# Row transposes by DMA, masks by ScalarE and new orders in a decoder layer of one core

## The chip, the core and the metric

The kernel runs on one core of a Trainium2 chip. TensorE, VectorE, ScalarE, GpSimd and SyncE each run their own list of instructions in order and meet at semaphores; TensorE writes to eight PSUM banks of 128 x 512 f32, and SyncE's list here only issues DMAs. The metric is the device time of one execution in microseconds. The kernel before takes 849.58 us, the median of 3 runs (848.94 to 849.9).

## What is computed

A decoder layer on x of 8 x 128 x 512, f32, with the normalisation behind each residual sum:

```python
x = _layernorm(x + _L0_attn_ref(x, Wq, bq, ..., Wo, bo), axis=-1)       # 32 heads of 16, causal
x = _layernorm(x + _L0_xattn_ref(x, ctx, ctx, mask, wq, wk, wv, wo), axis=-1)  # 32 query, 8 key heads of 128, rotary
x = _layernorm(x + _L0_ffn_ref(x, gate..., up..., down...), axis=-1)    # 4-bit weights, 1376 wide, f16 result
```

Products are made in f16 from a high and a low half of each operand (three matmuls in place of one), so that each f32 tensor is split: the high half is a cast, the low half the difference.

## The kernel before, in words

**Tiles.** Every engine's program is a loop over tile numbers t. Self-attention has STEPS1 = 64 tiles (t = 0 to 63: eight blocks j of 8 tiles; one tile is 4 heads of one batch of half the rows). T0 = 70 begins cross-attention, 64 tiles v = t - T0 of one batch and one group of 4 query heads, 16 blocks of 4. END = T0 + 64 begins the feed-forward part: four early gate and up products, then the coded tiles (weights of 7 of 11 column groups multiplied as codes), then the down products, batch by batch.

**Self-attention tile t.** TensorE: `scores1(t)` puts the causal mask into a bank by a matmul of a bf16 identity with the bf16 table `tri` (start=True) and adds two score matmuls; then projections of later blocks, or a fill; `weigh1(t - 3)`; `turn1(t - 1)` (four f32 transposes of the probabilities); every second tile one transpose of a normalised result. VectorE: row maximum of t, low half of the probabilities of t - 2 (`p1_lo`), normalisation of a result, then weights, then what the fills of tile t left in their bank. ScalarE: exponentials of t (they wait for the row maximum), high half of the probabilities of t - 1 (`p1_hi`), then projections and fills.

**Fills** (`fill_plan`, line 63) are projections, one or two a tile, that go to banks 0 and 1 in turn; fill f waits until fill f - 2 was consumed (`fill_free`). Kind "o" is the self-attention's output product of a batch (VectorE adds it to `res` and takes the statistics), "t" turns a batch's normalised rows into the columns `aTh`, `aTl` by four f32 transposes of TensorE, a cast by ScalarE and a subtraction by VectorE; "k", "v", "q" are the cross-attention's projections of a block; a "k" or "q" is rotated: VectorE makes three products (`rotation_parts`), GpSimd their sum (`rotation_sum`), ScalarE and GpSimd its halves, with two buffers. Before, tiles 52 to 58 hold k0; o0; o1; t0, o2; t1, o3; t2, v0; t3; and q0 to q3 follow in tiles 59 to 62, k1 in 63, v1 in 64, the queries of block 1 from 65 on. A "q" waits until the four rows tiles of its half are turned.

**Normalisation.** GpSimd makes the inverse deviation (`inverse_sd`) one tile behind the "o" fill. For batches in SHIFTED (4 to 7 of the first norm) it also makes a shift column, and ScalarE applies both; for the others VectorE does (`normalised`).

**Weights.** GpSimd splits the pieces of the first two cross-attention groups (`split_piece`: scale, cast, subtract) in the slots of QKV_SLOT (tiles 54 to 59 for group 1) and OUT_SLOT (50, 52, 60, 61). Self-attention weights of block 2 are split by ScalarE and VectorE in tiles 2 to 5.

**Joint.** In T0 + 2 stand the fills t4, k2, t5; in T0 + 3 t6 and t7. ScalarE takes t5 out of its bank behind the third exponentials; VectorE behind `o_lo(0)`.

**Down weights.** CODES_SLOT names the tiles in which codes are unpacked (VectorE) and scaled (GpSimd, `scale_codes`); column groups 4 and 5 have their down weights split in the coded tiles (`weights_hi` on ScalarE, `down_lo` on GpSimd).

## Time and profile before

| | |
|---|---|
| median of 3 runs | 849.58 us |
| the profiled execution's own time | 849.92 us |
| its span, first to last instruction | 848.1 us |
| TensorE busy | 98% |
| VectorE, GpSimd, ScalarE busy | 81%, 75%, 63% |
| granted TensorE clock, mean | 0.999 of full |
| DMA | 76.8 MB, 91 GB/s |
| chain that ended last | TensorE 62%, GpSimd 14%, VectorE 7%, ScalarE 7% |

Times in a timeline are microseconds from the start of the span: the start, the length, the engine, the line, what is written from what, how many alike; brackets give idle time ahead of it and what ended it. L356 to L358 are the three matmuls of the helper that all projections use, L1667 the transposes of probabilities, L1655 the causal mask, L1734 the transposed rows, L1155 any low half on VectorE.

### The profile page before, as it was taken

What the parts mean: (1) busy time and instruction counts of PE and PEld (TensorE: products, weight loads), DVE (VectorE), ACT (ScalarE), POOL (GpSimd) and SP (SyncE); (2) the same over time, 40 slices, a digit from 0 to 9 for tenths busy, and PEclk for the clock granted to TensorE, in tenths of its full rate; (3) what the DMA queues carried; (4) which work ended last, traced back from release to release, by engine and by line L of the source; (5) the groups of instructions that cost most, each with busy time, mean ns of one, the idle gap of its engine ahead of it and who ended that gap; (6) DMA issues with size and microseconds to landing.
All of it is one profiled execution on the core that took longest, in us unless ns stands there. A gap on an engine that the chain in (4) does not pass through costs nothing.

```text
span 848.1 us, 17377 instructions
## 1 busy us (share of the span) xinstructions
PE 827.7 (98%) x6125; PEld 465.5 (55%) x6125; DVE 689.2 (81%) x1077; ACT 533.6 (63%) x1560; POOL 632.8 (75%) x563
## 2 busy tenths in 40 slices
PE   9899999999999999999999999999999999999997
PEld 4677777655555554555555555555555644434444
DVE  5688788998688778689788788798889755899897
ACT  5798888554765666576575676665666753777400
POOL 1199999897676686578777677578888633999896
PEclk9999999999999999999999999999999999999999
DMA  7675255103244422434425125213442223230011
GB/s 192 194 256 181 63 160 163 54 18 108 38 95 130 112 39 75 112 39 138 105 38 155 33 40 161 38 26 91 133 93 39 46 42 105 72 110 20 2 48 52
DMA packets 120038, 76.76 MB, mean 91 GB/s; under 512 B 72877, under 2 KB 104336, under 8 KB 119952
## 3 DMA queue, kind: packets, MB, share of 16 engines
q1 hardware_dynamic: 117504, 74.86, 33.5%
q10 hardware_dynamic: 2448, 0.79, 0.5%
q8 instruction: 49, 0.80, 0.4%
q14 instruction: 37, 0.30, 0.1%
HBM read 52.50 MB, written 6.36 MB: 69 GB/s over the span
## 4 chain that ended last, share of the span: by engine, by line
PE 62%; POOL 14%; DVE 7%; ACT 7%; issue 6%; DMA 3%; SPq 0%; POOLq 0%; ACTq 0%; DVEq 0%
PE bank L356 16%; PE bank L358 16%; PE bank L357 16%; POOL rot L647 2%; POOL left L680 2%; PE bank L1667 2%; POOL q2l L653 2%; POOL pn L664 2%; ACT prob L845 2%; POOL prob L657 2%; PE bank L1840 1%; PE bank L1841 1%; PE bank L1760 1%; PE bank L1759 1%; PE bank L1758 1%
## 5 line engine op out<-in xcount | busy, mean ns | idle before, releaser
L657 POOL TENSOR_TENSOR prob<-prob,rden 128x512 f32<-128x512 f32 x64 | 67.8, 1060 | 103.3 <-DVE rden L1318 103.0
L647 POOL TENSOR_TENSOR rot<-rcos,rsin 128x512 f32<-128x512 f32 x80 | 106.5, 1332 | 20.3 <-DVE rsin L1260 19.8
L356 PE MATMUL bank<-aTh,xqh 128*128 128x512 f16 x256 | 97.1, 379 | 1.4 <-DVE rsin L1260 0.9
L356 PE MATMUL bank<-xoh,o2h 128*128 128x512 f16 x256 | 97.1, 379 | 0.1
L357 PE MATMUL bank<-xol,o2h 128*128 128x512 f16 x256 | 97.2, 379 | 0.0
L358 PE MATMUL bank<-xoh,o2l 128*128 128x512 f16 x256 | 97.1, 379 | 0.0
L357 PE MATMUL bank<-aTl,xqh 128*128 128x512 f16 x256 | 97.1, 379 | 0.0
L358 PE MATMUL bank<-aTh,xql 128*128 128x512 f16 x256 | 97.1, 379 | 0.0
L1010 ACT ACTIVATE prob<-bank,ebias 128x128 f32<-128x128 f32 x256 | 90.4, 365 | 2.1
L1260 DVE SCALAR_TENSOR_TENSOR rsin<-bank,sinq 64x512 f32<-64x512 f32 x128 | 88.1, 688 | 1.7
L664 POOL TENSOR_TENSOR pn<-prob,pn 128x512 f16<-128x512 f32 x64 | 84.1, 1315 | 6.8 <-ACT pn L1022 6.6
L653 POOL TENSOR_TENSOR q2l<-rot,q2h 128x512 f16<-128x512 f32 x64 | 82.0, 1282 | 0.0
L890 ACT CAST q2h<-rot 128x512 f16<-128x512 f32 x64 | 39.5, 618 | 61.8 <-POOL rot L647 61.4
L796 ACT ACTIVATE ebias<-nmax 128x4 f32<-128x4 f32 x128 | 27.0, 211 | 79.3 <-DVE nmax L1313 51.1
L845 ACT ACTIVATE prob<-bank,ebias 128x128 f32<-128x128 f32 x256 | 73.0, 368 | 2.1
L1155 DVE SCALAR_TENSOR_TENSOR o2l<-bank,o2h 128x512 f16<-128x512 f32 x64 | 43.5, 680 | 37.1 <-ACT o2h L796 36.8
L1022 ACT CAST pn<-prob 128x512 f16<-128x512 f32 x64 | 39.4, 615 | 52.6 <-POOL prob L657 52.4
L1260 DVE SCALAR_TENSOR_TENSOR rcos<-bank,cosq 128x512 f32<-128x512 f32 x64 | 43.7, 683 | 22.4 <-PE bank L358 22.4
L1179 DVE TENSOR_REDUCE nmax<-bank 128x4 f32<-128x512 f32 x64 | 43.7, 684 | 17.5 <-PE bank L1658 16.9
L1010 ACT ACTIVATION_READ_ACCUMULATOR prob<-bank,ebias 128x1 f32 x256 | 51.9, 203 | 0.0
L1332 DVE SCALAR_TENSOR_TENSOR res<-bank,res 128x512 f32<-128x512 f32 x64 | 43.8, 685 | 8.7 <-PE bank L358 8.3
L1155 DVE SCALAR_TENSOR_TENSOR pT<-bank,pT 128x512 f16<-128x512 f32 x64 | 43.8, 685 | 6.8 <-ACT pT L796 6.3
(224 smaller groups left out, 2652.7 us busy)
## 6 DMA issues: line engine op xcount, KB each, us to landing
tst<-tables SPq DMA_DIRECT2D x11, 768.0 KB, 5.2
xqs<-in_xwq SPq DMA_DIRECT2D x8, 1024.0 KB, 6.6
xos<-in_xwo SPq DMA_DIRECT2D x8, 1024.0 KB, 5.6
qst<-in_fq SPq DMA_DIRECT2D x11, 384.0 KB, 3.4
kstk<-stack SPq DMA_DIRECT2D x48, 64.0 KB, 2.3
qstk<-stack SPq DMA_DIRECT2D x21, 128.0 KB, 2.6
xs<-in_ctxT SPq DMA_DIRECT2D x2, 1024.0 KB, 6.3
res<-in_x SPq DMA_DIRECT2D x1, 2048.0 KB, 8.4
```

Of the source, the lines that this page charges most:

```text
L356: pe.matmul(out_ap, ah, bh, start=first, stop=False)
L357: pe.matmul(out_ap, ah, bl, start=False, stop=False)
L358: return pe.matmul(out_ap, al, bh, start=False, stop=last)
L647: nc.gpsimd.tensor_tensor(rot[:, r % 2, :], rcos[:, r % 2, :], rsin[:, r % 2, :], ALU.add).then_inc(rope_rot, 1)
L653: nc.gpsimd.tensor_tensor(lo, rot[:, r % 2, :], hi, ALU.subtract).then_inc(rope_lo, 1)
L657: nc.gpsimd.tensor_tensor(prob[:, v % 2, :].rearrange("p (h k) -> p h k", h=QH), prob[:, v % 2, :].rearrange("p (h k) -> p h k", h=QH), rd ...
L664: nc.gpsimd.tensor_tensor(pn[:, v % 2, 1, :], prob[:, v % 2, :], pn[:, v % 2, 0, :], ALU.subtract).then_inc(c_pn_lo, 1)
L845: last = nc.scalar.activation(prob[:, u % 2, j * S:(j + 1) * S], bank[2 + u % 2][:, j * S:(j + 1) * S], ACT.Exp, bias=ebias[:, u % 2, j:j ...
L1010: last = nc.scalar.activation(prob[:, v % 2, j * S:(j + 1) * S], bank[2 + v % 2][:, j * S:(j + 1) * S], ACT.Exp, bias=ebias[:, v % 2, j:j ...
L1155: return nc.vector.scalar_tensor_tensor(out=dst, in0=src, scalar=2.0 ** e, in1=hi, op0=ALU.mult, op1=ALU.subtract)
L1260: last = nc.vector.scalar_tensor_tensor(out=as_batches(dst[to, r % 2, :]), in0=as_batches(bank[f % 2][src, :]), scalar=2.0 ** (e - E_X - E_W),
L1332: nc.vector.scalar_tensor_tensor(out=r, in0=bank[6 + v % 2][:, :], scalar=2.0 ** (-E_V2 - E_W), in1=r, op0=ALU.mult, op1=ALU.add).then_inc ...
```

## The change

The four "t" fills of batches 0 to 3 go. Their rows are normalised by ScalarE (SHIFTED now holds all eight batches, so GpSimd makes four more shift columns), split as rows: high half by ScalarE (`split_rows_hi`), low half by VectorE (`split_rows_lo`) at the end of its tile, into a buffer of three places, and SyncE issues two DMA transposes for each batch into `aTh` and `aTl` (`turn_rows`). The first half's query fills wait for these DMAs. The fills become o0 to o3 in tiles 52 to 55, v0 in 56, k0 in 57, none in 58; the rest stays. In tiles 56 to 63 the causal mask is put into the bank by a copy on ScalarE, two tiles ahead and behind the exponentials of the running tile, and TensorE's mask matmul goes. In the opening two of three weight pieces of block 2 go to GpSimd, tiles 1 and 2, and block 1's queries leave their bank ahead of the exponentials of tile 0. In T0 + 2 ScalarE takes t5 out of its bank behind `o_hi(0)`, ahead of the exponentials, and VectorE its low half ahead of `o_lo(0)`. The codes of column group 5 are unpacked and scaled in END + 1 instead of END + 4, and the down weights of groups 4 and 5 split in END + 1 to END + 3 instead of in the coded tiles.

Left out here are declarations of semaphores, the size of `lnsh`, and a condition that keeps the early down weights out of ScalarE's coded loop.

```diff
@@ -58,15 +58,15 @@
 END = T0 + STEPS
+SEEDED = STEPS1 - 8
...
-    plan = [(STEPS1 - 12, "k", (0,)), (STEPS1 - 11, "o", (0,)), (STEPS1 - 10, "o", (1,)), (STEPS1 - 9, "t", (0, 0))]
-    plan += [(STEPS1 - 9, "o", (2,)), (STEPS1 - 8, "t", (0, 1)), (STEPS1 - 8, "o", (3,)), (STEPS1 - 7, "t", (0, 2))]
-    plan += [(STEPS1 - 7, "v", (0,)), (STEPS1 - 6, "t", (0, 3))]
+    plan = [(STEPS1 - 12 + b, "o", (b,)) for b in range(BH)]
+    plan += [(STEPS1 - 8, "v", (0,)), (STEPS1 - 7, "k", (0,))]
@@ -133,7 +133,7 @@
-W1_SLOT = {(3, 0): 7, (3, 1): 9, (3, 2): 10}
+W1_SLOT = {(2, 1): 1, (2, 2): 2, (3, 0): 7, (3, 1): 9, (3, 2): 10}
@@ -146,7 +146,7 @@
 APPLY_SLOT.update({(1, b): T0 + BH * (BLOCK_OF[(G - 1, b // BH)]) + b % BH + 5 for b in range(NB)})
-SHIFTED = [(0, b) for b in range(BH, NB)]
+SHIFTED = [(0, b) for b in range(NB)]
@@ -179,8 +179,9 @@
+DOWN_EARLY = {4: END + 1, 5: END + 2}
 EARLY_GU = {END: 1, END + 2: 2, END + 4: 3}
-CODES_SLOT = {0: T0 + 26, 1: T0 + 48, 2: T0 + 49, 3: T0 + 53, 4: END, 5: END + 4}
+CODES_SLOT = {0: T0 + 26, 1: T0 + 48, 2: T0 + 49, 3: T0 + 53, 4: END, 5: END + 1}
@@ -281,6 +282,9 @@
+        rows = at(155.5, "rows", [P, 3, 2, D], F16)
@@ -449,6 +455,13 @@
                 sp.dma_start(xos[:, :, :], xwo.rearrange("(h p) n -> p h n", p=P)[:, g * QH:(g + 1) * QH, :]).then_inc(xo_in, 16)
+            def turn_rows(b):
+                if b == 0:
+                    sp.wait_ge(v1_psum, BLOCKS)
+                for i, (dst, done) in enumerate(((aTh, rows_hi), (aTl, rows_lo))):
+                    sp.wait_ge(done, b + 1)
+                    sp.dma_start_transpose(dst[:, :, b * S:(b + 1) * S], rows[:, b % 3, i, :]).then_inc(rows_in[b % 3], 16)
@@ -528,6 +541,8 @@
             load_kv(1)
+            for b in range(BH):
+                turn_rows(b)
@@ -583,18 +598,21 @@
-            def split_piece(hi, lo, src, lo_done, e=E_W):
+            def split_piece(hi, lo, src, lo_done, e=E_W, ahead=None):
...
                 pool.wait_ge(piece_hi, pieces_done)
+                if ahead is not None:
+                    pool.wait_ge(lo_done, ahead)
...
                 pool.wait_ge(w1_in, 48 * (c - 1))
-                split_piece(w1h[c][:, i, :, :], w1l[c][:, i, :, :], w1s[0][:, i, :, :], w1_lo)
+                split_piece(w1h[c][:, i, :, :], w1l[c][:, i, :, :], w1s[0][:, i, :, :], w1_lo,
+                            ahead=3 * c + i)
@@ -723,7 +741,7 @@
                 for (norm, b), slot in APPLY_SLOT.items():
-                    if norm == layer and slot == t + 1 and (norm, b) not in SHIFTED:
+                    if norm == layer and slot == t + 1 and (layer == 1 or slot < T0):
@@ -770,11 +788,14 @@
                         inter_lo(n)
+                for i in DOWN_EARLY:
+                    if DOWN_EARLY[i] + 1 == t:
+                        down_lo(i)
...
                 add_left(n, 1)
-                if half == 1 and i in DOWN_SPLIT:
+                if half == 1 and i in DOWN_SPLIT and i not in DOWN_EARLY:
@@ -833,6 +854,14 @@
+            def split_rows_hi(b):
+                act.wait_ge(ln_out, b + 1)
+                if b == 0:
+                    act.wait_ge(v1_psum, BLOCKS - 1)
+                if b >= 3:
+                    act.wait_ge(rows_in[b % 3], 32 * (b // 3))
+                split_hi(rows[:, b % 3, 0, :], res[:, b, :], E_X).then_inc(rows_hi, 1)
@@ -855,6 +884,13 @@
+            def seed_triangle(u):
+                if u == SEEDED:
+                    act.wait_ge(consts_ready, 4)
+                act.wait_ge(exp_done, u - 1)
+                nc.scalar.copy(bank[2 + u % 2][:, :].rearrange("p (h k) -> p h k", h=4),
+                               tri[:, :].unsqueeze(1).to_broadcast([P, 4, S])).then_inc(seeded1, 1)
@@ -960,23 +996,37 @@
             w1_split_hi(0, 2)
+            def scaled_norm(layer, b):
+                e, r = layer * NB + b, res[:, b, :]
+                act.wait_ge(ln_shift, SHIFTED.index((layer, b)) + 1)
+                nc.scalar.activation(r, r, ACT.Identity, scale=lnrs[:, e % 3, :],
+                                     bias=lnsh[:, SHIFTED.index((layer, b)), :]).then_inc(ln_out, 1)
...
                 bank_splits(turned_first(t))
+                if t == 0:
+                    q1_out_f32(1)
...
                     exps1(t)
+                if SEEDED <= t + 2 < STEPS1:
+                    seed_triangle(t + 2)
...
                     p1_hi(t - 1)
+                for layer, b in SHIFTED:
+                    if APPLY_SLOT[(layer, b)] == t:
+                        scaled_norm(layer, b)
+                        split_rows_hi(b)
...
                         w1_split_hi(1, i)
-                if j + 1 < BLOCKS and n == 0 and t >= -TILES1:
+                if j + 1 < BLOCKS and n == 0 and t >= -TILES1 and t != 0:
@@ -984,20 +1034,14 @@
                     bring_first_queries()
-                if t in (2, 3, 4):
-                    w1_split_hi(2, t - 2)
+                if t == 2:
+                    w1_split_hi(2, 0)
...
                 rotations(fills_at(t - 1))
-            def scaled_norm(layer, b):
-                e, r = layer * NB + b, res[:, b, :]
-                act.wait_ge(ln_shift, SHIFTED.index((layer, b)) + 1)
-                nc.scalar.activation(r, r, ACT.Identity, scale=lnrs[:, e % 3, :],
-                                     bias=lnsh[:, SHIFTED.index((layer, b)), :]).then_inc(ln_out, 1)
@@ -1097,6 +1141,7 @@
                     o_hi(0)
+                    turned_hi(find_fill("t", 0, 5))
@@ -1109,7 +1154,8 @@
                 bank_splits([f for f in fills_at(t)[:1] if FILLS[f][1] == "t" and f not in turned_first(t)])
-                bank_splits([f for f in fills_at(t)[1:] if f not in turned_first(t)])
+                if v != 2:
+                    bank_splits([f for f in fills_at(t)[1:] if f not in turned_first(t)])
@@ -1123,6 +1169,9 @@
                             inter_hi(n)
+                for i in DOWN_EARLY:
+                    if DOWN_EARLY[i] == t:
+                        weights_hi(i)
@@ -1237,6 +1286,10 @@
                          E_X).then_inc(fill_free, 1)
+            def split_rows_lo(b):
+                dve.wait_ge(rows_hi, b + 1)
+                split_lo(rows[:, b % 3, 1, :], res[:, b, :], rows[:, b % 3, 0, :], E_X).then_inc(rows_lo, 1)
@@ -1442,8 +1495,8 @@
                 apply_norms(t)
-                if t in (3, 4, 5):
-                    w1_split_lo(2, t - 3)
+                if t == 3:
+                    w1_split_lo(2, 0)
@@ -1461,6 +1514,9 @@
                         consume(f)
+                for b in range(BH):
+                    if APPLY_SLOT[(0, b)] == t:
+                        split_rows_lo(b)
@@ -1481,6 +1537,8 @@
                     o_lo(0)
+                    early += [find_fill("t", 0, 5)]
+                    consume(early[-1])
@@ -1652,11 +1710,15 @@
                 dst = bank[2 + u % 2][:, :].rearrange("p (h k) -> p h k", h=4)
-                pe_.matmul(dst, identb[:, :], tri[:, :].unsqueeze(1).to_broadcast([P, 4, S]), start=True, stop=False)
+                if u >= SEEDED:
+                    pe.wait_ge(seeded1, u - SEEDED + 1)
+                else:
+                    pe_.matmul(dst, identb[:, :], tri[:, :].unsqueeze(1).to_broadcast([P, 4, S]), start=True, stop=False)
...
                     last = pe_.matmul(dst[:, 2 * i:2 * i + 2, :], qstk[0:3 * ROWS, j % 2, pair, t],
-                                      kstk[0:3 * ROWS, j % 2, :, pair, t], start=False, stop=(i == 1))
+                                      kstk[0:3 * ROWS, j % 2, :, pair, t], start=False, stop=(i == 1),
+                                      skip_group_check=(u >= SEEDED))
@@ -1708,7 +1770,11 @@
                 if kind == "q":
-                    pe.wait_ge(fill_free, find_fill("t", 0, BH * ORDER[n][1] + BH - 1) + 1)
+                    if ORDER[n][1] == 0:
+                        for place in range(3):
+                            pe.wait_ge(rows_in[place], 32 * len(range(place, BH, 3)))
+                    else:
+                        pe.wait_ge(fill_free, find_fill("t", 0, NB - 1) + 1)
...
                                    aTh, aTl, cols)

```

## Rows read from the trace of the kernel before

**Rows 1.** page, part 1: busy us of each engine, share of the span, instructions

```profile
PE 827.7 (98%) x6125; PEld 465.5 (55%) x6125; DVE 689.2 (81%) x1077; ACT 533.6 (63%) x1560; POOL 632.8 (75%) x563
```

**Rows 2.** table of stretches: us, each engine's busy us (instructions), granted clock, DMA

```profile
140.00:210.00 70.00, 67.83 (x633) 42.95 (x631) 61.01 (x109) 37.90 (x107) 61.46 (x62) 1.00 0.21 65
720.00:790.00 70.00, 67.69 (x303) 27.53 (x302) 61.44 (x77) 53.49 (x92) 65.92 (x50) 1.00 0.21 66
```

**Rows 3.** TensorE's waits over the whole run: total us, times, longest us

```profile
PE bank L1667 <- ACT prob L845: 2.1, 4, 1.1
...
PE bank L1734 <- DVE res L1225: 1.4, 2, 1.0
```

**Rows 4.** timeline of TensorE, tiles 55 and 56: start us, us, what, count

```profile
154.29 0.38 PE L1655 MATMUL bank<-tri,identb 128*128 128x512 bf16 x1
...
156.01 0.64 PE L1667 MATMUL bank<-ident,prob 128*128 128x128 f32 x4
...
156.48 0.38 PE L356 MATMUL bank<-woTh,oTh 128*128 128x512 f16 x1
...
157.13 0.38 PE L356 MATMUL bank<-woTh,oTh 128*128 128x512 f16 x1
```

**Rows 5.** timeline of ScalarE, tile 63 and one normalisation

```profile
186.88 0.20 ACT L796 ACTIVATE ebias<-nmax 128x4 f32<-128x4 f32 x1 [1.63 <-DVE nmax L1179]
187.11 1.14 ACT L845 ACTIVATE prob<-bank,ebias 128x128 f32<-128x128 f32 x4
188.34 0.59 ACT L864 CAST bank<-mbias 128x512 f32<-128x512 bf16 x1
188.87 0.59 ACT L796 ACTIVATE pT<-bank 128x512 f16<-128x512 f32 x1
...
218.13 0.80 ACT L999 ACTIVATE res<-res,lnsh,lnrs 128x512 f32<-128x512 f32 x1
```

**Rows 6.** timeline of VectorE, tiles 52 to 55

```profile
146.62 0.68 DVE L1260 SCALAR_TENSOR_TENSOR rcos<-bank,cosk 128x512 f32<-128x512 f32 x1
...
148.74 0.69 DVE L1179 TENSOR_REDUCE nmax<-bank 128x4 f32<-128x512 f32 x1
...
155.01 0.68 DVE L1232 SCALAR_TENSOR_TENSOR res<-bank,res 128x512 f32<-128x512 f32 x1
...
156.56 0.67 DVE L1179 TENSOR_REDUCE nmax<-bank 128x4 f32<-128x512 f32 x1
157.14 0.68 DVE L1155 SCALAR_TENSOR_TENSOR aTl<-bank,aTh 128x512 f16<-128x512 f32 x1
```

**Rows 7.** timeline of GpSimd, tiles 52 to 70; in brackets idle before, and releaser

```profile
150.30 1.27 POOL L647 TENSOR_TENSOR rot<-rcos,rsin 128x512 f32<-128x512 f32 x1
...
171.98 1.49 POOL L589 TENSOR_SCALAR xks<-xks 128x512 f32<-128x512 f32 x1
...
175.35 1.49 POOL L589 TENSOR_SCALAR xvs<-xvs 128x512 f32<-128x512 f32 x1
...
199.27 1.27 POOL L647 TENSOR_TENSOR rot<-rcos,rsin 128x512 f32<-128x512 f32 x1 [1.47 <-DVE rsin L1260]
...
212.28 0.27 POOL L721 TENSOR_SCALAR lnsh<-lnmv,lnrs 128x1 f32<-128x1 f32 x1
```

**Rows 8.** timeline of GpSimd, coded tiles: the low half of a down weight

```profile
738.97 1.15 POOL L697 TENSOR_TENSOR wdl<-deq,wdh 128x512 f16<-128x512 f32 x1
```

**Rows 9.** DMA issues: count, median us from issue to landing

```profile
pT<-pn SPq DMA_TRANSPOSE x64, 3.1
```

**Rows 10.** timeline of TensorE: three starts that the sum goes by

```profile
171.94 0.38 PE L356 MATMUL bank<-aTh,xqh 128*128 128x512 f16 x1 [0.37 <-DVE aTl L1155]
...
194.30 0.38 PE L356 MATMUL bank<-aTh,xqh 128*128 128x512 f16 x1
...
228.12 0.66 PE L1734 MATMUL bank<-ident,res 128*128 128x128 f32 x4 [0.76 <-DVE aTl L1155]
```

**Rows 11.** waits of VectorE from 718 to 790: total us, times, longest us

```profile
DVE total L1388 <- POOL left L680: 4.4, 4, 1.8
```

More of the change, by code:

```diff
@@ L231, in decoder_kernel @@
         power = sb("power", [P, 1], F32)
-        lnsh = sb("lnsh", [P, BH, 1], F32)
+        lnsh = sb("lnsh", [P, NB, 1], F32)
         scol16 = sb("scol16", [P, (NI - NSPLIT) * 2 * NK], F16)
@@ L321, in decoder_kernel @@
         k1_out, q1_out, q1_first, stack_in = sem("k1_out"), sem("q1_out"), sem("q1_first"), [sem("stack_in0"), sem("stack_in1")]
+        seeded1 = sem("seeded1")
         s_psum, nmax_done, ebias_done, exp_done = sem("s_psum"), sem("nmax_done"), sem("ebias_done"), sem("exp_done")
@@ L327, in decoder_kernel @@
             sem("ln_sum"), sem("ln_stat"), sem("ln_aggr"), sem("ln_ve"), sem("ln_rs"), sem("ln_out"))
+        rows_hi, rows_lo, rows_in = sem("rows_hi"), sem("rows_lo"), [sem(f"rows_in{i}") for i in range(3)]
         ln_shift, ln_mid, ln_right = sem("ln_shift"), sem("ln_mid"), sem("ln_right")
@@ L1138, in _ @@
                     woven_hi(j)
-                if half == 0 and i in DOWN_SPLIT:
+                if half == 0 and i in DOWN_SPLIT and i not in DOWN_EARLY:
                     weights_hi(i)
```

## The prediction

> **What bounds the kernel now.** I read the page's busy times first: TensorE is busy 98% of the span, 827.7 of 848.1 us [rows 1]. The reader is to see that little is idle there, so a change gains by taking work off TensorE or by closing a few named waits, and it loses wherever it makes TensorE wait for a slower chain. The table of stretches comes next: from 140 to 210 us, where most of the change lies, TensorE is busy 67.8 of 70 us, but GpSimd 61.5 and VectorE 61.0; from 720 to 790, GpSimd is busy 65.9 and VectorE 61.4 [rows 2]. In both stretches other engines are nearly full too, so taking work from TensorE alone may give nothing. Among TensorE's waits are 1.4 us for two normalisations, and none for another compute engine is over 1.1 us [rows 3].
>
> **Prices.** For TensorE starts are the right measure, since a matmul's listed length overlaps the next. Four 128-column f32 transposes take 156.48 - 156.01 = 0.47 us; three 512-column matmuls take 157.13 - 156.48 = 0.65, so 0.216 each, and a fill of twelve 2.6 [rows 4]. The Trainium skill (Trainium Kernel Development and Optimization, Performance Expectations) calls matmul busy time a bad measure of how near a kernel is to its limit; the listed x4 of 0.64 us against 0.47 [rows 4] agrees. Priced by listed lengths, the sixteen transposes and eight mask matmuls that go would be 2.6 + 3.0 us instead of 1.9 + 1.7.
>
> ScalarE in a self-attention tile [rows 5]: exponent bias 0.23; four exponentials, until something that waits for them starts, 1.23; a 128x512 mask copy into a bank 0.53; a probability high half about the same, 0.49 to 0.53; a normalisation by scale and bias 0.80, and 0.84 with the wait for its own end. VectorE [rows 6]: row maximum 0.58 to the next start, 0.67 until its result is there; a low half, of the same listed length, 0.60; a rotation's three products 148.74 - 146.62 = 2.1; residual sum with statistics 156.56 - 155.01 = 1.55. GpSimd [rows 7]: a weight piece 175.35 - 171.98 = 3.37, a rotation sum 1.24 to 1.27, the new shift column 0.27 behind the two small steps of about 1.0 that stay; a rotated low half is the subtraction that takes 1.15 elsewhere [rows 8]. A DMA transpose lands 3.1 us after its issue [rows 9]; it has twice the columns of the new ones, so 3.1 is my value and the upper end, and 0 the lower, as nothing else is on that queue then.
>
> **Part 1, opening.** The second block's queries leave their bank ahead of the first exponentials instead of behind them. ScalarE is idle there, so the copy, 0.5 us at the price of the mask copy, leaves the path of the second tile. Two of three weight pieces of block 2 go to GpSimd, idle there too, and are wanted 5 and 10 us later; at 3.4 us each they cost nothing, and if GpSimd were late, TensorE would wait for block 2's queries. I take **-0.4**, between -1.0 (its relief reaches block 2's keys as well) and 0.
>
> **Part 2, self-attention tiles 52 to 63.** Off TensorE go 4 x 0.47 = 1.9 us of transposes, 8 x 0.216 = 1.7 of mask matmuls, and waits: from tile 55's mask at 154.29 [rows 4] to the first query fill at 171.94 [rows 10] are 17.65 us, with 15.3 of work in them (three fills 7.8, transposed tiles 1.9, the tiles' own parts 5.6), so 2.3. That is **-5.9**, if nothing else came late. But look at the order of what replaces them. In tiles 53 to 56 VectorE ends with the rows' low half; it waits for the high half, which on ScalarE stands behind that tile's exponentials, the seed, the probability half and the normalisation; and those exponentials wait for the row maximum with which VectorE starts the same tile. So one tile takes 0.67 + 0.23 + 1.23 + 0.53 + 0.49 + 0.84 + 0.62 + 0.60 and some 0.1 of hand-over = **5.3 us**, where TensorE has 3.6 to 3.8 us of work. In tile 56 the high and low halves of the first value fill stand in the same row: 6.4.
> Walked in order: tile 53's row maximum starts at 148.2 (148.74, less 2.1 - 1.55, as a sum with statistics now runs ahead of it). GpSimd turns to the first inverse deviation at 150.3, where its rotation was [rows 7]; so shift column 151.6, normalisation 152.4, high half 153.1, and with the low half the next row maximum at 153.7. Then tile 55 at 159.0, tile 56 at 164.3, tile 57 at 170.7. TensorE is through with tile 57 at 167, and in tile 58 it must wait for a probability low half that VectorE makes only after tile 57's row maximum: until 171.9, an idle of **4.8 us**. Exponentials of tile 57 end at 172.9, transposes and scores at 173.7. The last rows' low half is written at 170.6, so its transpose lands by 173.7 at the latest: hardly a further wait. The first query fill starts at 173.7 instead of 171.94: **+1.8** and not -5.1, which is the end if there is no such lockstep.
> Behind that GpSimd decides. It works in order, and the rotation sum of k0, now in tile 57, waits for VectorE until 174.0, with two pieces queued behind it. Then, without a break: sum 1.24, two pieces 6.7, low half 1.15, sum 1.24, piece 3.37, sum 1.24, piece 3.37, low half 1.15, sum 1.24 = 20.7, so the sum of the third query head ends at 194.7. VectorE's products of k1 need that buffer (196.8), and TensorE's next query fill needs their bank; the exponentials of tile 63 stand on ScalarE behind that head's copy too. That fill starts at 197.2 instead of 194.30 [rows 10]: **+2.9**; the four masks saved in between are lost in the wait. GpSimd's own slack begins at 197.8 [rows 7], too late. Without the queue those four masks would bring +1.8 down to +0.9. Ends +0.9 and, should the head's copy hold up ScalarE longer, +4.
>
> **Part 3, joint.** Batch 5's transposed tile leaves its bank ahead of the third exponentials. The wait of 0.76 us at 228.12 [rows 10] goes, but VectorE's low half of it now stands ahead of the first context's low half, which the first output product needs 0.6 earlier; ScalarE's exponentials start 0.5 later. Net **-0.5** at the next query fill, between -1.0 and +0.6.
>
> **Part 4, down tiles.** GpSimd loses two low halves of down weights, 1.15 us each at the least [rows 8], from the coded tiles; ScalarE loses two high halves. With the codes of tile 5 they go behind the last exponentials, where VectorE and GpSimd wait for late transposes: free there, and up to 0.6 if they push one. In the coded tiles VectorE waits 4.4 us for GpSimd's sums, in 4 waits [rows 11]. With 2.3 us of GpSimd's work gone I take **-2.3**. Ends: -0.4, if VectorE, at 61.4 of 70 us, has to fill in for itself; -3.0.
>
> **The sum.** -0.4 + 2.9 - 0.5 - 2.3 = -0.3. The profiled execution took 849.92 us, its span of 848.1 and 1.8 around it, 0.34 above the median of 849.58. So the median comes to 849.3.
>
> **Rivals.** (a) *Only the first wait holds*: GpSimd catches up before k1's products, so +0.9 stands for +2.9: 847.3. For it speaks that it has idle spots from 197.8 on [rows 7]; against it, that the 20.7 us have no hole. (b) *TensorE's own sum decides*: -5.9 - 0.4 - 0.5 - 2.3 = -9.1: 840.5. ScalarE and VectorE would have to overlap what I put in a row; that each step waits for the one before speaks against it. (c) *Slower: VectorE is the bound of the coded tiles.* It is busy there 61.4 of 70 us [rows 2]; if its own work sets when banks come free, part 4 gives 0.4 instead of 2.3, and with part 2 at its upper end: -0.4 + 4 - 0.5 - 0.4 = +2.7: 852.3. It decides from the point where VectorE has no idle left ahead of its sums. (d) *The clock falls*: the granted clock is 1.00 in both stretches [rows 2], the 2.4 GHz level; a wait of 4.8 us is new, the longest for a compute engine being 1.1 [rows 3]. At 1.2 GHz a fill would take 2.6 us more, part of it hidden by GpSimd: +1 to +3, so 851.5. The Trainium skill (TensorE: Matmul & The Clock Gate, Why this matters for your kernels) warns that idle gaps between bursts of matmuls, if long, send the array back to the slow clock; by that rule this case would come. (e) *The change doesn't do what it says*: the queries' fill would have to get its rows from elsewhere; its waits name the DMA's semaphores, so I give this nothing.
>
> **How the numbers follow.** Forecast 0.42 at 849.3, its own range 847.8 to 851.2; (a) 0.24; (b) 0.10; (c) 0.16; (d) 0.08. The range leaves out (b) and the far side of (c) and (d), and takes in some of what lies between (a) and (b): 845.0 to 852.3. About 0.2%, 1.7 us, is what a measurement of this kernel can tell from no change. Faster by more: (b), most of (a), a little of the forecast, 0.38. Slower: (c), (d), 0.24. Between: 0.38.
>
> **What would show it.** Right: a TensorE wait of 4 to 5 us in tile 58 for a probability low half; row maxima of tiles 54 to 57 5.3 us apart; GpSimd without idle from 174 to 195 us; the first query fill of block 1 at 197; fewer of VectorE's waits for GpSimd's sums in the coded tiles. Wrong: those row maxima less than 4.5 us apart (then (b) or (a)); a wait for the row transposes; a granted clock under 1.00 behind the gap; TensorE's waits for sums in the coded tiles unchanged.

## The result, and the profile after

The changed kernel takes 852.9 us in the median of 6 runs (851.48 to 853.32), the kernel before 849.74 beside it (6 runs, 848.94 to 850.17): ratio 1.0033, 95% interval 1.0023 to 1.0043. Forecast were 849.3, with 845.0 to 852.3: too low, and the kernel is slower where hardly a change was forecast. Four executions of 952 to 2877 us (two of the kernel before, one of opening_only, one of orders) are left out of the ratios below. The profiled execution took 853.32 us, its span 851.5.

Page of the changed kernel, part 1, beside [rows 1]; then its table of stretches, beside [rows 2] (engine busy us, instructions, granted clock, DMA):

```profile
PE 825.7 (97%) x6101; PEld 465.1 (55%) x6101; DVE 687.9 (81%) x1071; ACT 541.4 (64%) x1570; POOL 641.4 (75%) x573
```

```profile
140.00:210.00 70.00, 63.02 (x592) 40.13 (x591) 54.81 (x98) 45.24 (x119) 59.69 (x62) 0.93 0.28 80
720.00:790.00 70.00, 68.15 (x308) 28.20 (x307) 59.88 (x75) 51.73 (x87) 61.92 (x47) 1.00 0.17 57
```

TensorE has less to do and is idle 7 us of the first stretch, where it was idle 2.2; the clock, 1.00 before, is 0.93 there. Its waits from 140 to 210 us (total us, times, longest us), beside [rows 3]:

```profile
PE bank L1744 <- DVE pT L1204: 5.3, 1, 5.3
PE bank L1744 <- DVE onrm L1244: 1.3, 1, 1.3
PE bank L1729 <- ACT prob L874: 0.3, 1, 0.3
```

The 5.3 us are the predicted wait of tile 58 (forecast 4.8). Where the time came from is read best between fixed points on TensorE: the first transposed output of self-attention (start to A), the 21st of the 32 (B), the first query fill of block 1 (C), the third query fill of block 2 (D), score tile 60 of cross-attention (E) and the last matmul (F). In the expectations B is once called the transposed output of tile 44, once the eleventh, once named after a product of block 6; it is always this point. Each letter's column is the stretch that ends there. Lengths in us, each from the difference of two starts in one profiled execution; in the last column the ratio to the kernel before, with its interval:

```
               A      B      C      D       E       F    ratio to before
before       38.52  93.76  62.02  45.07  429.15  173.60
changed      37.86  95.46  66.34  44.50  428.92  172.52   1.0033 (1.0023-1.0043)
no_opening   37.91  93.57  66.76  44.47  428.87  172.51   1.0029 (1.0019-1.0039)
part2_only   37.87  93.86  67.12  44.91  429.03  173.49   1.0053 (1.0040-1.0067)
opening_only 37.65  93.38  62.03  45.08  429.61  173.48   0.9999 (0.9990-1.0009)
warm         37.83  94.02  66.35  44.49  429.09  172.52   1.0032 (1.0021-1.0044)
warm_out     38.24  95.22  64.68  45.05  428.86  172.49   1.0021 (1.0011-1.0031)
masks_back   39.12  94.91  64.40  44.46  429.26  172.49   1.0015 (1.0006-1.0025)
piece_later  37.57  95.37  68.81  46.05  428.95  172.51   1.0080 (1.0067-1.0094)
codes_only   38.56  94.33  66.24  44.45  429.04  173.50   1.0043 (1.0028-1.0057)
high_halves  37.47  93.37  66.68  44.46  428.87  173.45   1.0049 (1.0034-1.0065)
unlocked     37.74  95.48  62.30  44.49  428.69  172.51   0.9986 (0.9976-0.9995)
orders       38.18  94.89  63.17  44.50  429.01  172.50   1.0001 (0.9992-1.0010)
orders_out   37.51  94.96  61.69  44.96  428.86  172.50   0.9959 (0.9947-0.9972)
orders_warm  37.26  93.34  60.28  45.02  428.86  172.50   0.9959 (0.9945-0.9974)
orders_warm2 38.07  93.26  61.73  45.03  429.13  172.47   0.9961 (0.9945-0.9976)
best         38.38  93.59  59.91  45.02  428.87  172.49   0.9960 (0.9948-0.9973)
```

From before to changed: A -0.66, B +1.70, C +4.32, D -0.57, E -0.23, F -1.08, together +3.5. C is part 2, D the joint, F the down tiles. D and F repeat to 0.1 or so among kernels that are alike there, E to 0.9; A and B do not.

C depends a little on where GpSimd stands at B. Its first inverse deviation (lnve) starts 18.19 us behind B in the changed kernel and 18.15 to 20.49 behind it in the experiments on that kernel, and it lies ahead of all that they alter between B and C. So differences in C of under 1 us say little by themselves. Counted from that deviation to the end of C: 48.1 us in changed, warm and codes_only, 47.7 to 47.8 in no_opening, part2_only and high_halves, 50.7 in piece_later, 46.5 in warm_out, 45.3 in masks_back, 44.1 in unlocked, 44.2 in orders, 42.7 in orders_out, 41.2 in orders_warm2, 41.0 in orders_warm and best.

The lockstep of C, as VectorE's timeline shows it in the changed kernel (start us, us; in brackets the idle time and who ended it):

```profile
159.61 0.70 DVE L1204 SCALAR_TENSOR_TENSOR rows<-res,rows 128x512 f16<-128x512 f32 x1 [1.44 <-ACT rows L817]
160.24 0.68 DVE L1228 TENSOR_REDUCE nmax<-bank 128x4 f32<-128x512 f32 x1
...
164.98 0.69 DVE L1204 SCALAR_TENSOR_TENSOR rows<-res,rows 128x512 f16<-128x512 f32 x1 [1.93 <-ACT rows L817]
165.59 0.68 DVE L1228 TENSOR_REDUCE nmax<-bank 128x4 f32<-128x512 f32 x1
...
171.32 1.58 DVE L1204 SCALAR_TENSOR_TENSOR rows<-res,rows 128x512 f16<-128x512 f32 x1
172.82 0.68 DVE L1228 TENSOR_REDUCE nmax<-bank 128x4 f32<-128x512 f32 x1
```

Each row maximum (nmax) waits behind a low half of the rows, which waits for ScalarE: 160.24, 165.59, 172.82, so 5.35 us apart as forecast (5.3), and then 7.23 where 6.4 was. The last low half took 1.58 us instead of 0.69; that is the first surprise. GpSimd at that time and behind it:

```profile
171.20 1.16 POOL L610 TENSOR_TENSOR xql<-xqs,xqh 128x512 f16<-128x512 f32 x1
176.18 1.26 POOL L665 TENSOR_TENSOR rot<-rcos,rsin 128x512 f32<-128x512 f32 x1 [3.82 <-DVE rsin L1313]
...
195.80 1.26 POOL L665 TENSOR_TENSOR rot<-rcos,rsin 128x512 f32<-128x512 f32 x1
```

From 176.18 to 197.06, the end of the third query head's sum, it has no hole: 20.9 us, forecast 20.7. And TensorE behind its gap:

```profile
176.09 0.63 PE L1719 MATMUL bank<-kstk,qstk 96*128 96x256 f16 x2
176.52 0.63 PE L362 MATMUL bank<-aTh,xqh 128*128 128x512 f16 x1
176.94 0.63 PE L363 MATMUL bank<-aTl,xqh 128*128 128x512 f16 x1
...
199.66 0.38 PE L362 MATMUL bank<-aTh,xqh 128*128 128x512 f16 x1
```

The first query fill has starts 0.43 us apart instead of 0.216 [rows 4] until 179.5, the 1.2 GHz level: rival (d) came true too. The query fill of block 1 starts at 199.66, 5.36 later than in [rows 10].

### The profile page after: what moved, and what is told of

Read it like the earlier page. It is cut to its first block, busy times and chain, and to the rows that moved or that the text cites. A ratio compares the mean times of both kernels' runs of the same rounds, so it can differ in the third digit from the quotient of the medians.

```text
span 851.5 us, 17400 instructions
## 1 busy us (share of the span) xinstructions
PE 825.7 (97%) x6101; PEld 465.1 (55%) x6101; DVE 687.9 (81%) x1071; ACT 541.4 (64%) x1570; POOL 641.4 (75%) x573
## 4 chain that ended last, share of the span: by engine, by line
PE 64%; POOL 12%; ACT 7%; DVE 7%; issue 6%; DMA 3%; SPq 0%; POOLq 0%; DVEq 0%; ACTq 0%
PE bank L362 16%; PE bank L364 16%; PE bank L363 16%; POOL rot L665 3%; PE bank L1729 2%; ACT prob L874 2%; PE bank L1906 2%; POOL q2l L671 2%; POOL pn L682 2%; PE bank L1907 2%; POOL prob L675 2%; PE bank L1892 1%; DVE nmax L1228 1%; PE bank L1826 1%; PE bank L1825 1%
## 5 line engine op out<-in xcount | busy, mean ns | idle before, releaser
L1204 DVE SCALAR_TENSOR_TENSOR o2l<-bank,o2h 128x512 f16<-128x512 f32 x64 | 43.5, 680 | 37.3 <-ACT o2h L817 36.0
```

Of the source, the lines that this page charges most:

```text
L1204: return nc.vector.scalar_tensor_tensor(out=dst, in0=src, scalar=2.0 ** e, in1=hi, op0=ALU.mult, op1=ALU.subtract)
```

## Experiments

Their names stand in the table above.

### The clock and GpSimd's queue

**warm.** The changed kernel with 30 extra matmuls where TensorE waits.

```diff
+                if t == STEPS1 - 6:
+                    for _ in range(30):
+                        pe_.matmul(bank[5][:, 136:512], cTh[:, 0, 0:P], cTh[:, 0, 0:376], start=True, stop=True)
                 if 3 <= t <= STEPS1 + 2:
                     weigh1(t - 3)
```

> The changed kernel with 30 more matmuls of 376 columns (4.7 us at full clock) into unused columns of a bank in tile 58, right where TensorE waits 5.3 us for VectorE; their results are used by nothing. Both theories: the granted clock stays at 1.00 from 170 to 180 us, and the first query fill starts about 0.9 us earlier (175.6) and takes 2.6 instead of 4.1 us. Theory 1, GpSimd's queue decides: the query fill of block 1 comes only 0 to 0.5 us earlier than 199.66, and the time is 852.4 to 852.9. Theory 2, the clock decides: it comes 2.3 us earlier, and the time is 850.6.

Stretches of the changed kernel, then of this one:

```profile
170.00:175.00 5.00, 0.52 (x13) 0.43 (x13) 4.27 (x6) 2.08 (x8) 2.20 (x3) 0.50 0.26 52
175.00:180.00 5.00, 5.00 (x17) 2.65 (x18) 3.96 (x8) 4.14 (x11) 3.67 (x4) 0.55 0.00 0
```

```profile
170.00:175.00 5.00, 4.10 (x36) 2.44 (x35) 4.94 (x7) 2.46 (x7) 1.18 (x2) 1.00 0.51 55
175.00:180.00 5.00, 5.00 (x39) 2.71 (x37) 3.98 (x9) 4.47 (x14) 4.85 (x5) 1.00 0.00 0
```

The clock stays at 1.00, and the second query fill starts 2.1 us earlier, counted from B. Yet C is 66.35 us, against 66.34: theory 1 holds. The clock fell, and it cost nothing at the end of C, since the queue hides it. The 851.75 us in all are 0.1 below the changed kernel by the ratios.

**warm_out.** The same, with two output-weight pieces out of the queue.

```diff
-    out = {0: [50, 52, 60, 61], 1: [T0 + 2, T0 + 3, T0 + 4, T0 + 5]}
+    out = {0: [50, 52, 62, 64], 1: [T0 + 2, T0 + 3, T0 + 4, T0 + 5]}
```

> The changed kernel with the 30 extra matmuls in tile 58 and with two output-weight pieces moved on GpSimd from tiles 60 and 61 to 62 and 64. With the matmuls alone the clock stayed up and the first query fill ended 3.5 us earlier, but from the transposed output of tile 44 to the query fill of block 1 it took 66.35 us, as in the changed kernel (66.34; 62.02 before). Theory (GpSimd's queue took that gain): with two pieces out of the queue this stretch is 63.9 to 64.6 us and the time 2 us under that of the kernel with the matmuls alone. Rival (something else in tiles 59 to 64 binds): 66.3 again, no gain.

C is 64.68, 1.7 us less than in warm, a little short of the 1.8 to 2.5 expected: the queue had been setting its end. The two pieces late without the extra matmuls were not run, so how much of the 1.7 needs the clock is not shown. D is longer by 0.55 us, as in every kernel with these two pieces late, so by the ratios 0.9 us of the 2 expected are left.

**piece_later.** The changed kernel with GpSimd's piece of tile 57 behind the first rotation sum: one more piece in the queue, and the neighbour of the long low half gone.

```diff
-           1: [54, 55, 56, 57, 58, 59]}
+           1: [54, 55, 56, 58, 58, 59]}
```

> The changed kernel with the weight piece of tile 57 moved on GpSimd to tile 58, behind the first rotation sum. There the subtraction of this piece ran from 171.20 for 1.16 us beside VectorE's last low half of the rows, which took 1.58 instead of 0.69 us. Theory 1 (an instruction of VectorE with all operands in SBUF does not run while GpSimd's does): that low half takes 0.7 us, the row maxima of tiles 56 and 57 are 6.3 to 6.4 us apart instead of 7.2, TensorE's wait in tile 58 is 4.4 instead of 5.3 us. Rival: 1.58 us has another cause and stays. Theory 2 (GpSimd's queue decides the query fill of block 1): it has one more piece of 3.4 us in it behind the rotation sum, which comes 0.9 us earlier, so that the stretch from the transposed output of tile 44 to that fill is 68.8 instead of 66.3 us, and the time 855.4. Rival: the stretch shrinks with the wait, to 65.4.

VectorE, and TensorE's wait, in this kernel:

```profile
165.14 0.68 DVE L1228 TENSOR_REDUCE nmax<-bank 128x4 f32<-128x512 f32 x1
...
170.87 0.68 DVE L1204 SCALAR_TENSOR_TENSOR rows<-res,rows 128x512 f16<-128x512 f32 x1
171.47 0.69 DVE L1228 TENSOR_REDUCE nmax<-bank 128x4 f32<-128x512 f32 x1
```

```profile
PE bank L1744 <- DVE pT L1204: 4.4, 1, 4.4
```

The low half takes 0.68 us, the maxima are 6.33 apart, the wait is 4.4: GpSimd's subtraction had held VectorE for 0.9 us. And C is 68.81 where 68.8 was expected: the queue sets it. (D is 1.6 longer, so the whole is 856.4.)

### The lockstep

**masks_back.** The last eight masks on TensorE again.

```diff
-SEEDED = STEPS1 - 8
+SEEDED = STEPS1
```

> The changed kernel with the masks of the last eight self-attention tiles on TensorE again instead of seeds on ScalarE. Theory: the seed is one of the steps in a row of a tile, 0.53 us; without it row maxima of tiles 53 to 56 are 4.8 instead of 5.3 us apart, TensorE's wait in tile 58 is 3 to 3.7 instead of 5.3 us, GpSimd's queue starts 2.1 us earlier, and the first query fill of block 1 comes 1.5 to 2.1 us earlier: 851.0. The four masks behind it on TensorE (0.87 us) are hidden by GpSimd's queue. Rival: TensorE's own work counts, the masks cost it 1.7 us, and the time stays at 852.9 or above.

C is 64.40, 1.94 less than in the changed kernel, as the theory had it, and 2.4 less than in no_opening and high_halves, counted from the first deviation, which stands there as it does here. So of the 4.3 us of C the seeds are about half. The row maxima of tiles 54 to 56 are 4.6 us apart instead of 5.3, so each seed cost 0.7 us of its tile, not the 0.53 of the price, for 1.7 us of TensorE's work that nothing waited for.

**unlocked.** The changed kernel with VectorE's low half of the rows one tile later, behind the next tile's row maximum and probability low half.

```diff
                 if 2 <= t <= STEPS1 + 1:
                     p1_lo(t - 2)
+                for b in range(BH):
+                    if APPLY_SLOT[(0, b)] == t - 1:
+                        split_rows_lo(b)
...
-                for b in range(BH):
-                    if APPLY_SLOT[(0, b)] == t:
-                        split_rows_lo(b)
```

> The changed kernel with VectorE's low half of a row block made one tile later, behind the next tile's row maximum and probability low half, so that the row maximum no longer stands behind the normalisation. Theory: the chain of row maximum, exponentials, seed, high half, normalisation, rows' high half and low half in one tile is what takes 5.3 us; broken, ScalarE's own 4 us decide, row maxima of tiles 53 to 57 are 3.9 to 4.3 us apart, TensorE's wait of 5.3 us in tile 58 shrinks to under 1.5, the granted clock stays at 1.00, and the first query fill of block 1 starts at 195 to 197: 848.5 to 850. Rival: ScalarE and GpSimd are too full anyway; the row maxima stay over 5 us apart and the time within 0.5 us of 852.9.

VectorE's maxima of tiles 54 to 56 and 57 in this kernel:

```profile
153.28 0.67 DVE L1228 TENSOR_REDUCE nmax<-bank 128x4 f32<-128x512 f32 x1
...
157.04 0.67 DVE L1228 TENSOR_REDUCE nmax<-bank 128x4 f32<-128x512 f32 x1
...
160.59 0.67 DVE L1228 TENSOR_REDUCE nmax<-bank 128x4 f32<-128x512 f32 x1
...
167.33 0.69 DVE L1204 SCALAR_TENSOR_TENSOR v2l<-bank,v2h 128x512 f16<-128x512 f32 x1 [3.95 <-ACT v2h L817]
167.94 0.68 DVE L1228 TENSOR_REDUCE nmax<-bank 128x4 f32<-128x512 f32 x1
```

Those of tiles 54 to 56 are 3.6 to 3.8 us apart, not 5.3; to that of tile 57 it is still 7.35. One instruction of the tile moved gives back 4.0 of the 4.3 us, and the kernel is the first one faster than the one before (847.86 against 849.42 us, interval below 1). The step that failed in the expectation: TensorE still waits 2.5 us in tile 58, since the maximum of tile 57 stands behind the value fill's low half; 1.1 us follow for the last row transpose, and the clock still falls (0.996 over the run).

**orders, orders_out.** On top of unlocked, whose lines are left out here, VectorE takes that low half behind the maximum of tile 57, GpSimd the fourth deviation ahead of a piece; then also two pieces late.

```diff
-                inverse_sds(0, t - 1)
+                if t != STEPS1 - 8:
+                    inverse_sds(0, t - 1)
+                if t == STEPS1 - 9:
+                    inverse_sd(BH - 1)
                 pieces(t)
...
+                if t == STEPS1 - 7:
+                    consume(find_fill("v", 0))
...
-                    if f not in turned_first(t):
+                    if f not in turned_first(t) and t != STEPS1 - 8:
                         consume(f)
```

> The kernel with the low half of the rows one tile later (847.9, against 849.4 of the kernel before), and two more orders: VectorE takes the low half of the first value fill behind the next tile's row maximum instead of ahead of it, and GpSimd computes the fourth inverse deviation ahead of the weight piece of tile 55 instead of behind it. In that kernel TensorE still waits 2.5 us in tile 58, for a row maximum behind that low half, and 1.1 us for the last row transpose, which stands behind the deviation. Theory: both waits shrink to under 0.5 us each and the first query fill starts 3 us earlier in the stretch, with the granted clock at 1.00. But GpSimd's queue of eight weight pieces and its sums then decides alone: the query fill of block 1 gains 0 to 1 us, 847.3. Rival: TensorE decides, and it gains 3 us: 844.9.

> The same with two output-weight pieces of group 0 moved on GpSimd from tiles 60 and 61 to 62 and 64. Theory (GpSimd's queue decides in the kernel without this): the query fill of block 1 comes 2 to 3 us earlier than there, 844.9 to 845.5. Rival (TensorE decides there): no change against it.

Both missed. In orders two waits of 1.0 us (exponentials) and 1.9 us (the last row transpose) are left, and behind them the first query fill runs whole at the low clock, 6.14 us to the next fill instead of 3.8. C is 63.17, longer than the 62.30 of unlocked, but neither the waits nor the clock make that difference: the second query fill starts 44.03 us behind B in both. GpSimd's first deviation, in unlocked and in orders:

```profile
151.41 0.23 POOL L734 TENSOR_SCALAR lnve<-lnmv 128x1 f32<-128x1 f32 x1
```

```profile
152.04 0.23 POOL L734 TENSOR_SCALAR lnve<-lnmv 128x1 f32<-128x1 f32 x1
```

Behind B that is 18.20 and 18.97 us, 0.8 later ahead of anything that orders alters. The first rotation sum follows at 38.82 and 39.72, and from there both need 23.5 us to the end of C. So the queue still sets it, and the two new orders gave nothing there. Why the eleven runs of each are 1.3 us apart is not shown. In orders_out C is 61.69, 1.5 less than in orders, not 2 to 3. Its medians say 3.1 less (847.07 against 850.14), but its profiled execution, 848.20, was the slowest of its six; the fastest, 845.21, was the one whose clock stayed at 1.000. The stretches of the profiled one:

```profile
165.00:170.00 5.00, 2.51 (x39) 1.97 (x37) 3.81 (x6) 3.45 (x9) 4.85 (x5) 0.89 0.27 53
170.00:175.00 5.00, 5.00 (x13) 1.65 (x13) 2.44 (x6) 3.67 (x11) 4.85 (x5) 0.50 0.00 0
```

**orders_warm, orders_warm2.** Extra matmuls, 5 and 7 of 512 columns, ahead of the transposes of tile 58 and of the first query fill, on top of orders_out; in the second one the pieces are in 62 and 63.

```diff
+                if t == STEPS1 - 5:
+                    pe.wait_ge(fill_free, find_fill("q", 0, 0) - 1)
+                    for _ in range(7):
+                        pe_.matmul(bank[find_fill("q", 0, 0) % 2][:, :], cTh[:, 0, 0:P], cTh[:, 0, 0:512], start=True, stop=True)
                 for f in fills_at(t)[:1]:
                     fill(f)
...
+                if t == STEPS1 - 6:
+                    for _ in range(5):
+                        pe_.matmul(turn_bank(t - 1)[:, :], cTh[:, 0, 0:P], cTh[:, 0, 0:512], start=True, stop=True)
                 if 1 <= t <= STEPS1:
                     turn1(t - 1)
```

> The kernel with all orders (low half of the rows a tile later, value fill's low half and fourth deviation reordered, two output-weight pieces late), with 5 and 7 extra matmuls of 512 columns where TensorE waits 1.1 us for exponentials and 1.4 us for the last row transpose; their results are used by nothing. Without them the granted clock was 0.50 for some 5 us behind these two waits and the first query fill took 5.1 instead of 2.6 us. Theory 1 (the clock falls for the lack of work in these waits, and nothing hides it now): clock 1.00 there, and the stretch from the transposed output of tile 44 to the query fill of block 1 is 59.6 to 60.4 us instead of 61.69: 845.2 beside 847.1. Theory 2 (hidden by GpSimd's queue again): 61.7, no gain.

> The same with the second output-weight piece in tile 63 instead of 64. With tile 64 TensorE waits 1.1 us for the second score tile of cross-attention and the joint part gained 0.1 instead of 0.6 us. Theory: GpSimd's piece in tile 64 stood ahead of what the first exponentials there need; in tile 63 the joint is 0.5 us shorter again, and the rest is the same. Rival: the query fill of block 1 comes later by the same 0.5 us.

The clock is 1.00, the step from first to second query fill 3.58 us instead of 6.32, and C 60.28, 1.4 less than in orders_out (1.7 counted from the first deviation). Now that less stands in the queue the clock costs something. In the times this is not to be told apart: both ratios are 0.9959. orders_warm2 missed: D is the same 45.03, so tile 64 was not what lengthened it. C is 1.45 longer, but that doesn't bear the rival out: GpSimd's first deviation starts 1.21 us later behind B and the first rotation sum 1.43 later, both ahead of the piece that was moved; counted from the deviation C is 0.2 longer. What costs D its 0.5 us is open.

### The opening and the down tiles

**no_opening, opening_only, best.** The opening undone in the changed kernel; alone in the kernel before; undone in orders_warm.

```diff
-W1_SLOT = {(2, 1): 1, (2, 2): 2, (3, 0): 7, (3, 1): 9, (3, 2): 10}
+W1_SLOT = {(3, 0): 7, (3, 1): 9, (3, 2): 10}
...
-                if t == 0:
-                    q1_out_f32(1)
...
-                if j + 1 < BLOCKS and n == 0 and t >= -TILES1 and t != 0:
+                if j + 1 < BLOCKS and n == 0 and t >= -TILES1:
...
-                if t == 2:
-                    w1_split_hi(2, 0)
+                if t in (2, 3, 4):
+                    w1_split_hi(2, t - 2)
```

> The changed kernel with the opening part undone (the second block's queries leave their bank behind the exponentials again, and ScalarE and VectorE split all three weight pieces of block 2). Theory: the opening gains 0.6 us and gives back 1.7 us at 62 to 82 us of the span, because GpSimd's extra pieces shift its work against VectorE's, and VectorE's instructions with all operands in SBUF last longer when they fall together with GpSimd's. Then this kernel is 1.0 us under the changed one, 851.9, and TensorE's fill of tile 52 starts at 143.1 as before the change. Rival: the opening is a gain as predicted (0.4) and the 1.0 us come from elsewhere: then this kernel is 0.4 us over the changed one, 853.3.

> The kernel before with the opening part alone (second block's queries out of their bank ahead of the first exponentials; two weight pieces of block 2 on GpSimd). The four profiles with and without this part so far need 95.5, 95.5 and 94.0 us with it, 93.8, 93.6 and 93.9 without it from the first transposed output to the third output tile of block 6's first product (93.8 before). Theory: the part costs 0 to 1.7 us from execution to execution, 1.0 in the mean, because GpSimd's work falls otherwise beside VectorE's: 850.4 against 849.4 of the kernel before. Rival, as the prediction had it: 0.4 us less, 849.0. Rival 2: it does nothing, 849.4.

> The kernel with all orders and extra matmuls, and with the opening part undone. Over the profiles so far the stretch from the first to the eleventh transposed output took 93.3 to 95.5 us with the opening part (11 profiles, mean 94.5) and 93.6 to 93.9 without it (3 profiles). Theory (the part costs some 0.7 us in the mean through collisions of GpSimd and VectorE): 845.4 where the same kernel with the part has 846.1 (ratio to the kernel before 0.995 instead of 0.996). Rival (nothing, the spread is of single executions): 846.1; rival as predicted: 846.5.

By all runs the part does nothing that can be told: 1.0029 without it against 1.0033 with it, 0.9999 alone, 0.9960 against 0.9959. So rival 2, and "nothing" in the last, and my theory of 0.7 to 1.0 us fell. A is 37.3 to 39.1 us with the part and 37.9 to 38.5 without, so the 0.66 of the changed kernel's profile are no gain of its own. B differs among executions of the same instructions (the changed kernel 95.46, warm 94.02; both are alike up to tile 58). B is above 94.8 in 7 of 13 profiles with the part and in none of 4 without, so a small loss there is possible, and not shown.

**part2_only.** Opening as above, and joint and down tiles undone.

```diff
-DOWN_EARLY = {4: END + 1, 5: END + 2}
+DOWN_EARLY = {}
...
-                    turned_hi(find_fill("t", 0, 5))
...
-                    early += [find_fill("t", 0, 5)]
-                    consume(early[-1])
```

The codes of tile 5 go back to `END + 4`.

> Only the self-attention part of the change (DMA transposes of rows, their order, masks seeded by ScalarE); opening, joint and down tiles as before the change. Theory: it costs 4.3 us at the first query fill of block 1, and nothing later gives or takes: 849.7 + 4.3 = 854.0. Rival, as the prediction had it: 2.9 us, 852.6.

C is 67.12, 5.1 us more than before, and the ratio says 4.5 us: nearer to the theory than to the prediction. D shrinks by 0.16 only, so 0.4 of the joint's 0.57 are the joint's edit.

**codes_only, high_halves.** `DOWN_EARLY = {}` in the changed kernel; then only GpSimd's early low halves taken out.

```diff
-                for i in DOWN_EARLY:
-                    if DOWN_EARLY[i] + 1 == t:
-                        down_lo(i)
...
-                if half == 1 and i in DOWN_SPLIT and i not in DOWN_EARLY:
+                if half == 1 and i in DOWN_SPLIT:
                     down_lo(i)
```

> The changed kernel with the down weights' high and low halves of tiles 4 and 5 back in the coded tiles; only the codes of tile 5 stay early. From the score tile 60 of cross-attention to the last matmul every kernel with the down part took 1.08 to 1.10 us less than 173.6 us before, and 0.11 less without it. Theory: one wait of TensorE for VectorE's totals (0.6 us and the small ones round it) went because VectorE's and GpSimd's work on the codes of tile 5 had left that place, and the low halves on GpSimd never set it: 1.0 us less stays. Rival, as the prediction had it: GpSimd's low halves are what counts, and without them the gain is under 0.4 us.

> The changed kernel with GpSimd's low halves of the down weights of tiles 4 and 5 back in the coded tiles; ScalarE's high halves and the codes of tile 5 stay early. With high and low halves both back, the 1.1 us that the down part gives between the score tile 60 of cross-attention and the last matmul were gone (173.50 us against 172.52 and 173.60 before). Theory (GpSimd is what counts, as the prediction had it): 173.4 to 173.5 here. Rival (ScalarE's relief counts): 172.5.

TensorE's waits for VectorE's totals from 700 to 800 us: before, changed, and in high_halves:

```profile
PE bank L1840 <- DVE total L1388: 2.0, 4, 0.6
```

```profile
PE bank L1906 <- DVE total L1441: 1.6, 3, 0.6
```

```profile
PE bank L1903 <- DVE total L1438: 2.0, 4, 0.6
```

VectorE's waits for GpSimd's sums from 718 to 800 us, in the changed kernel and in high_halves; before they were 4.4 us in 4 waits, as in [rows 11]:

```profile
DVE total L1441 <- POOL left L698: 3.2, 3, 1.8
```

```profile
DVE total L1438 <- POOL left L698: 4.4, 4, 1.8
```

F is 173.50 and 173.45, hardly under the 173.60 before. My theory of codes_only fell. Without GpSimd's two early low halves hardly anything of the gain is left, as the prediction said: one wait of VectorE and one of TensorE go only with them. Whether they would do it with the codes of tile 5 in their old place was not run.

## Why the prediction was wrong

Two terms of the sum were mis-sized and one gain did not come: part 2 priced the low halves of the rows, which VectorE reads from SBUF, at 0.60 us as if they ran alone, where one took 1.5; part 4 took GpSimd's saved work of 2.3 us for time on the path, where 1.1 came; and part 1's 0.4 was not to be seen.

**Part 1 (-0.4).** Measured 0 with 0.9 either way. In the profiled execution A and B together have +1.04, which belongs to that execution; the median is 0.4 below it.

**Part 2 (+2.9): the mechanism right, the size 1.4 short.** Lockstep, wait in tile 58, queue without a hole, fill of block 1 behind it: each was there. The term came to +4.32. Counted from B, the first rotation sum started 1.14 us later than in the walk (42.86 against 174.0 - 132.28 = 41.72); 0.9 of it is the last low half, which I priced at 0.60 as if it ran alone; piece_later shows it. In no_opening, part2_only and high_halves the loss falls elsewhere: GpSimd's first deviation starts 18.9 to 19.3 us behind B (18.0 in the walk), the first two low halves take 0.9 and 1.0 us, the last one 0.68, and C is no shorter. The queue was 0.2 longer and the way from its end to the fill 0.1. The new transposes landed 2.5 us after their issue in the median, under the 3.1 that I took as upper end, and TensorE did not wait for them here. The sentence that the four masks saved behind the first fill are lost in the wait is borne out by warm: the 2.1 us gained there at the second query fill were lost too.

**Part 3 (-0.5).** -0.57 in D, 0.4 of it by the edit itself.

**Part 4 (-2.3): the mechanism right, the term mis-sized by 1.2.** I took GpSimd's 2.3 us of saved work for time on the path, from VectorE's waits of 4.4 us [rows 11]. The row that bounds it is one step further on, TensorE's own waits for those totals: 2.0 us in 4 waits. One of them went (0.4 by the view). By the starts 1.1 us went: 0.26 at 738.6 us of the kernel before, 0.17 at 739.4 and 0.55 at 744.7, where the view has that one wait, the smaller ones being in no row of it; and 0.13 at 690.8, which codes_only and high_halves have too.

**The sum.** -0.3 forecast; +0.4 for part 1, +1.4 for part 2, +1.2 for part 4 make +2.7, and +3.2 was measured; the 0.5 that is left belongs to no part that I can name.

**The rivals.** (a) fell with the queue, which had no hole, and (b) with the row maxima. (c) named the right sign and nearly the right time for the wrong reason: its part 4 end (-0.4) is not what came (-1.1), and part 2's +4 was put down to ScalarE. (d) came as a fact, with a gap of 5.3 us and behind it the 1.2 GHz level until 179.5 us, and the rule of the Trainium skill (TensorE: Matmul & The Clock Gate, Why this matters for your kernels), that long gaps between bursts of matmuls bring the slow clock back, had it right; but its price, +1 to +3, was 0 at the end of C, and for the reason that its own line gave for a part of it, "hidden by GpSimd". (e) fell.

**A kernel faster than both.** best and orders_warm keep DMA transposes and seeds and take 846.3 and 846.1 us, 0.4% less than the kernel before and 0.7% less than the changed one. What the change lacked was the place of one low half and a shorter queue on GpSimd; whether the two orders that came with orders are needed too is open, since unlocked with late pieces alone was not run.

## What to carry to other kernels

When work is moved from a full engine to others, write down each engine's order of one tile and look for an instruction that ends one engine's tile, waits for another engine's last step, and stands ahead of what starts the next tile: here it cost 4 us, and one tile's delay of it gave them back. Before you lay a small difference between two profiles at the door of an edit, find the first instruction that is late and see whether it stands ahead of the edit: in orders and orders_warm2 it did. Bound a gain by the waits of the engine that sets the end, not by those of an engine ahead of it. A lost clock level or a closed wait is worth nothing while a queue without a hole runs beside it, so ask of each term what would be late next.

## What the hardware showed

**VectorE with two SBUF operands and GpSimd.** In the changed kernel VectorE's low half of an output-weight piece (128x512, both operands in SBUF, 28 of them) took 0.68 us each time that GpSimd ran nothing of 128x512 beside it (7 times), and 0.68 to 2.60, 1.38 in the mean, beside such work (21 times). Low halves of the same size with one operand in PSUM took 0.66 to 0.69 in all 164 cases on that line, and the statistics, with one SBUF operand, 0.68 to 0.70 in all 23. It goes both ways: GpSimd's scaling of a piece took 1.99 us instead of 1.50 where a low half of the rows (164.98 above) had started just ahead of it:

```profile
165.06 1.99 POOL L604 TENSOR_SCALAR xqs<-xqs 128x512 f32<-128x512 f32 x1
```

The Trainium skill says so (SBUF — State Buffer, SBUF: two separate sides): VectorE and GpSimd share a pair of ports, which whoever comes first keeps for the whole instruction, a VectorE instruction with two SBUF inputs among them, against a GpSimd instruction that reads SBUF. The trace agrees: the last low half of the rows started 0.12 us behind GpSimd's subtraction (171.32 and 171.20) and ended 0.54 us after it (172.90 and 172.36). And the prediction should have weighed this: a low half that was read from a PSUM bank is now read from SBUF.

**The clock after short waits.** In orders_out no wait of TensorE was over 1.4 us; two of them, 1.1 and 1.4 us, with only small matmuls and transposes round them from 165.1 to 169.9 us, still stood ahead of 5 us at clock 0.50, and twelve extra matmuls in these waits kept it at 1.00 (165 to 170, then 170 to 175 us in orders_warm):

```profile
165.00:170.00 5.00, 4.37 (x23) 2.02 (x22) 4.91 (x10) 2.81 (x10) 4.69 (x6) 1.00 0.26 52
170.00:175.00 5.00, 5.00 (x39) 2.73 (x37) 3.99 (x7) 4.53 (x12) 4.85 (x5) 1.00 0.01 3
```
